# Causal attention: the row-maximum pass and the causal masks issued as four 128x32 column tiles, narrow diagonal blocks merged into one bank

## The reference: what is computed

```python
q, k, v = heads(x @ wq), heads(x @ wk), heads(x @ wv)   # 16 heads of 8 features
scores = einsum('bhqd,bhkd->bhqk', q, k)
scores = where(causal, scores, -inf)
attn = softmax(scores / sqrt(8), axis=-1)
ctx = einsum('bhqk,bhkd->bhqd', attn, v)
```

## Time and profile before

| | |
|---|---|
| time, median of 3 runs | 1314.45 us (1314.13 to 1315.17) |
| time of the profiled execution | 1314.37 us |
| its span in the profile | 1312.6 us |
| TensorE busy | 1186.3 us (90%), 8293 matmul records |
| TensorE weight loads | 461.7 us (35%) |
| VectorE busy | 1033.5 us (79%) |
| ScalarE busy | 668.8 us (51%) |
| GpSimd busy | 65.3 us (5%) |

### The profile page before, as it was taken

How to read it: one execution, slowest core, us unless ns; L and a number is a source line. 1 busy time by engine, 2 the same in 40 slices (tenths; PEclk the granted TensorE clock), 3 DMA queues, 4 the chain that set the end, 5 groups by cost and what they waited for, 6 DMA issues and landing times.

```text
span 1312.6 us, 21461 instructions
## 1 busy us (share of the span) xinstructions
PE 1186.3 (90%) x8293; PEld 461.7 (35%) x8293; DVE 1033.5 (79%) x2503; ACT 668.8 (51%) x861; POOL 65.3 (5%) x62
## 2 busy tenths in 40 slices
PE   1899968999999999999699979599999999999997
PEld 1455533222222222333355547232222222222336
DVE  8976487899999897875547566789999999877664
ACT  1322114555677667766332224145556667777663
POOL 5111010000000000000101000100000000000000
PEclk9999988999999999999799979799999999999999
DMA  4100141000000000000000000420000000000001
GB/s 147 33 1 1 48 121 57 1 2 1 2 1 1 2 1 1 1 1 2 1 0 1 1 0 25 146 57 1 1 2 1 1 1 1 1 1 2 1 2 33
DMA packets 23506, 23.26 MB, mean 18 GB/s; under 512 B 3134, under 2 KB 21220, under 8 KB 23404
## 3 DMA queue, kind: packets, MB, share of 16 engines
q1 hardware_dynamic: 22252, 18.73, 4.9%
q0 software_dynamic: 1152, 3.15, 0.9%
HBM read 13.20 MB, written 8.39 MB: 16 GB/s over the span
## 4 chain that ended last, share of the span: by engine, by line
PE 69%; DVE 25%; issue 2%; ACT 2%; DMA 1%; SPq 0%; DVEq 0%; ACTq 0%
PE psum L1182 19%; PE psum L1202 17%; DVE part_max L1317 14%; PE psum L442 9%; PE psum L1162 8%; PE psum L1169 4%; PE psum L466 2%; PE psum L898 2%; PE psum L1205 2%; PE psum L913 1%; DVE xn L167 1%; DVE norm_v L150 1%; PE psum L427 1%; DVE parts L838 1%; PE psum L1225 1%
## 5 line engine op out<-in xcount | busy, mean ns | idle before, releaser
L1317 DVE TENSOR_REDUCE part_max<-psum 128x1 f32<-128x512 f32 (+3 forms) x1280 | 703.5, 604 | 118.2 <-PE psum L1205 59.4
L1279 ACT ACTIVATE hidden<-psum 128x1024 f32<-128x1024 f32 (+3 forms) x640 | 542.4, 895 | 311.1 <-PE psum L1169 166.1
L1202 PE MATMUL psum<-k_slots,q_slots 128*128 128x512 f16 (+3 forms) x1280 | 396.8, 359 | 43.5 <-DVE part_max L1317 24.4
L1182 PE MATMUL psum<-hidden,v_aug 128*9 128x512 f32 (+3 forms) x2560 | 296.1, 535 | 0.0
L1202 PEld LDWEIGHTS psum<-k_slots,q_slots 128*128 128x128 f16 x1280 | 111.5, 97 | 402.0 <-DVE part_max L1317 320.0
L442 PE MATMUL psum<-parts,w_parts 128*128 128x512 f16 x768 | 177.6, 382 | 1.9 <-DVE parts L838 1.9
L1162 PE MATMUL psum<-q_slots,k_slots 32*128 32x512 f16 (+3 forms) x1280 | 163.9, 355 | 7.2 <-ACT hidden L1279 4.6
L1205 PE MATMUL psum<-ident_bf,later_keys 128*128 128x128 bf16 x512 | 111.0, 227 | 0.0
L442 PEld LDWEIGHTS psum<-parts,w_parts 128*128 128x128 f16 x768 | 73.2, 99 | 80.9 <-issue 3.0
L586 ACT CAST parts<-psum 128x512 f16<-128x512 f32 x64 | 37.2, 588 | 106.7 <-PE psum L427 106.7
L1162 PEld LDWEIGHTS psum<-q_slots,k_slots 32*128 32x128 f16 x1280 | 46.3, 91 | 109.4 <-issue 52.1
(11 more groups left out here) (168 smaller groups left out, 735.7 us busy)
## 6 DMA issues: line engine op xcount, KB each, us to landing
q_slots<-q_rows SPq DMA_DIRECT2D x8, 512.0 KB, 3.8
k_slots<-k_rows POOLq DMA_DIRECT2D x24, 128.0 KB, 4.1
q_rows<-parts SPq DMA_DIRECT2D x18, 128.0 KB, 2.7
k_rows<-parts SPq DMA_DIRECT2D x18, 128.0 KB, 2.4
q_slots<-in_L_ffn_W_dram SPq DMA_DIRECT2D x2, 1024.0 KB, 6.6
k_slots<-k_rows SPq DMA_DIRECT2D x8, 128.0 KB, 4.0
q_slots<-nm_parts SPq DMA_DIRECT2D x64, 4.0 KB
out_dram<-x_res SPq DMA_DIRECT2D x4, 256.0 KB, 2.3
```

Source lines behind the costliest of these rows:

```text
L1182: last = pe.matmul(psum[VW * h:VW * h + DH + 1, O_BANK, off:CH], v_aug[:, j, G * g + h, :], probs[:, (2 * n + h // 2) % NP, h % 2, off:CH] ...
L1202: last = pe.matmul(psum[:, bank, 0:w], q_slots[:, g, qb * P:(qb + 1) * P], k_slots[:, G * g + h, kc * CH:kc * CH + w], start=True, stop=kc ...
L1279: act.activation(probs[:, tile % NP, :, off:CH], psum[:, bank:bank + 2, off:CH], ACT.Exp, scale=scale).then_inc(exp_done, 1)
L1317: dve.tensor_reduce(dst, psum[:, bank, 0:w], axis=AX.X, op=ALU.max).then_inc(ring_read, 1)
```

## The change

1. `ring_item`: each maximum matmul, stationary 128x128, becomes four matmuls with stationary operands of 128x32 (32 queries each), moving the same keys, with their outputs on the four partition quarters of the bank. The mask matmul of a diagonal unit becomes four 128x32 ones likewise.
2. A diagonal unit of block 0 (128 wide) now holds 4 heads in one bank, one of block 1 (256 wide) 2 heads: 11 units per step on the diagonal in place of 16, 560 in a layer in place of 640. VectorE reduces such a bank with one instruction of 4 or 2 outputs, and one group of mask matmuls serves all heads of the bank.
3. The masks of the score tiles (`mask_tile`) are four 128x32 matmuls for each head, and are issued after both score tiles of the quad.
4. The ring items of a turn are cut in halves before and after `values`, no longer at three quarters.
5. `UNIT_FIXED, QUAD_FIXED` go from 64, 64 to 100, 500, and a unit's columns now count its mask: the number of units beside each quad shifts.

```diff
-        UNIT_FIXED, QUAD_FIXED = 64, 64
+        UNIT_FIXED, QUAD_FIXED = 100, 500
...
+                    heads = CH // unit_width(step, i, kc)
+                    units += [(step, i, kc, h, heads) for h in range(0, G, heads)]
...
+            return heads * (unit_width(step, i, kc) + (P if kc == step[1] else 0))
...
                                          start=True, stop=q not in diagonal)
-                    if q in diagonal:
-
-                        for par in range(2):
-                            last = pe.matmul(psum[:, S_BANKS + 2 * (tile % 2) + par, off:off + P],
-                                             ident_bf[:, :], later_keys[:, :], start=False, stop=True)
+                    if q not in diagonal:
+                        last.then_inc(scores_done, 1)
+
+                def mask_tile(q, pr):
+
+                    off = first_query(q)
+                    tile = 2 * quad_no[q] + pr
+                    for par in range(2):
+                        for m in range(COLS):
+                            last = pe.matmul(psum[rows32(m), S_BANKS + 2 * (tile % 2) + par, off:off + P],
+                                             ident_bf[:, rows32(m)], later_keys[:, :], start=False, stop=True)
                     last.then_inc(scores_done, 1)
...
-                        last = pe.matmul(psum[:, bank, 0:w], q_slots[:, g, qb * P:(qb + 1) * P],
-                                         k_slots[:, G * g + h, kc * CH:kc * CH + w], start=True, stop=kc < c)
+                        for a in range(heads):
+                            for m in range(COLS):
+                                last = pe.matmul(psum[rows32(m), bank, a * w:(a + 1) * w],
+                                                 q_slots[:, g, qb * P + m * SLOT:qb * P + (m + 1) * SLOT],
+                                                 k_slots[:, G * g + h0 + a, kc * CH:kc * CH + w],
+                                                 start=(a == 0), stop=(kc < c))
                         if kc == c:
-                            last = pe.matmul(psum[:, bank, i * P:w], later_keys[:, :], ident_bf[:, :],
-                                             start=False, stop=True)
+                            for m in range(COLS):
+                                last = pe.matmul(diagonal_part(psum[rows32(m), bank, 0:heads * w], heads),
+                                                 later_keys[:, rows32(m)], repeated(ident_bf, heads),
+                                                 start=False, stop=True)
...
-                    cuts = [0, 0, len(items) // 2 + len(items) // 4, len(items)]
+                    half = (len(items) + 1) // 2
                     if q:
                         score_tile(q, 0)
-                    for item in items[cuts[0]:cuts[1]]:
-                        ring_item(item)
-                    if q:
                         score_tile(q, 1)
-                    for item in items[cuts[1]:cuts[2]]:
+                    if q in diagonal:
+                        mask_tile(q, 0)
+                        mask_tile(q, 1)
+                    for item in items[:half]:
                         ring_item(item)
                     if previous:
                         values(previous)
-                    for item in items[cuts[2]:cuts[3]]:
+                    for item in items[half:]:
                         ring_item(item)
...
-                            dst = part_max[:, step_no[s] % 2, h, i, kc:kc + 1]
-                            w = CH if kc < s[1] else (i + 1) * P
-                            dve.tensor_reduce(dst, psum[:, bank, 0:w], axis=AX.X, op=ALU.max).then_inc(ring_read, 1)
+                            w = unit_width(s, i, kc)
+                            dve.tensor_reduce(part_max[:, step_no[s] % 2, h0:h0 + heads, i, kc],
+                                              psum[:, bank, 0:heads * w].rearrange("p (a k) -> p a k", a=heads),
+                                              axis=AX.X, op=ALU.max).then_inc(ring_read, 1)
```

More of the change, by code:

```diff
@@ L36 @@
 SLOT = 32
+COLS = P // SLOT
 MAX_ROW = TERMS * DH
@@ L1009, in macaron_layers, with unit_width @@
         SLACK = 3
-        UNIT_FIXED, QUAD_FIXED = 64, 64
+        UNIT_FIXED, QUAD_FIXED = 100, 500
         def quads_of(step):
             return [(step, j) for j in range(BPC * (step[1] + 1))]
+        def unit_width(step, i, kc):
+            return CH if kc < step[1] else (i + 1) * P
         def max_units_of(step):
-            return [(step, i, kc, h) for i in range(BPC) for kc in range(step[1] + 1) for h in range(G)]
+            units = []
+            for i in range(BPC):
+                for kc in range(step[1] + 1):
+                    heads = CH // unit_width(step, i, kc)
+                    units += [(step, i, kc, h, heads) for h in range(0, G, heads)]
+            return units
         def columns_of_quad(q):
@@ L1023, in columns_of_unit @@
         def columns_of_unit(u):
-            (_, c), i, kc, _ = u
-            return CH if kc < c else (i + 1) * P
+            step, i, kc, _, heads = u
+            return heads * (unit_width(step, i, kc) + (P if kc == step[1] else 0))
         def units_beside_quads():
@@ L1146, in attention_layer, with rows32, diagonal_part, repeated @@
                          for s in STEPS}
+            def rows32(m):
+                return slice(SLOT * m, SLOT * (m + 1))
+            def diagonal_part(rows, heads):
+                return rows.rearrange("p (a k) -> p a k", a=heads)[:, :, -P:]
+            def repeated(mask, heads):
+                return mask[:, :].rearrange("p (a k) -> p a k", a=1).broadcast_to([P, heads, P])
             @blk.tensor
@@ L1194, in ring_item @@
                     if kind == "scores":
-                        (g, c), i, kc, h = what
-                        if (g, i, kc, h) == (0, 0, 0, 0):
+                        (g, c), i, kc, h0, heads = what
+                        if (g, i, kc, h0) == (0, 0, 0, 0):
                             pe.wait_ge(q_landed[c], 16 if c else 16 * (G + 1))
@@ L1313, in _ @@
                         if kind == "scores":
-                            s, i, kc, h = what
-                            dst = part_max[:, step_no[s] % 2, h, i, kc:kc + 1]
-                            w = CH if kc < s[1] else (i + 1) * P
-                            dve.tensor_reduce(dst, psum[:, bank, 0:w], axis=AX.X, op=ALU.max).then_inc(ring_read, 1)
+                            s, i, kc, h0, heads = what
+                            w = unit_width(s, i, kc)
+                            dve.tensor_reduce(part_max[:, step_no[s] % 2, h0:h0 + heads, i, kc],
+                                              psum[:, bank, 0:heads * w].rearrange("p (a k) -> p a k", a=heads),
+                                              axis=AX.X, op=ALU.max).then_inc(ring_read, 1)
                         elif kind == "turned":
```

2 lines of the change are left out of this document (1 added, 1 removed).

## The result

The changed kernel takes 1227.73 us (median of 4 runs, 1224.66 to 1232.76) against 1314.29 us (4 runs, 1309.46 to 1315.17) for the kernel before. The ratio is 0.9352, 95% interval 0.931 to 0.9394: 6.5% less, some 85 us. Two further sets of runs of the same kernel gave ratios of 0.9333 and 0.9312.

What follows compares the result with a forecast made beforehand. The prediction took TensorE to set the pace, VectorE close behind in the first half. Relief kept, 26 us a layer less 1 for chunk 0, twice, gave 50 us off 1314: 1264 us, range 1244 to 1294.

Steps and rivals of the forecast that it cites:

- The price of a change of shape: TensorE: every change of matmul tile shape costs about 0.105 us; 763 changes a layer before, 355 after.
- A group of four tiles: Maximum and mask matmuls on TensorE: four 32-column f16 tiles of 512 columns run side by side in 0.22 us.
- Both slower rivals: TensorE: f16 strips no faster than f32, 1482 us, chance 0.07; matmul pairs can't be supplied, some 1450 us, chance 0.03.
- that of the narrow groups: Rival: 128-column groups held by four weight loads, or VectorE taking more; about 1285 us, 1279 to 1305, chance 0.16.
- The 5 ns a group on top: TensorE surcharge for each group of four column tiles, from weight-load starts 4 ns apart; 5.4 us a layer.
- ScalarE's idle time ahead of a diagonal quad: Wait before a diagonal quad's first exponential: about 0.65 us in the last steps, 1.15 us before the change.
- the sum: Six stages of a layer: net TensorE relief, cut where VectorE is nearly full, keeps 26 us, less 1 for chunk 0.
- Merging: Narrow diagonal units sharing a bank: fewer VectorE reductions save 0.4 us a step, or 6 us a layer.
- TensorE sets the pace: Attention stages before the change: TensorE's records cover 93 to 99% in the first three, with VectorE close behind.
- 0.3 us on some six turns and 1 us on two steps: ScalarE cost of later diagonal masks: some six 512- and 384-column turns from step (3,2) on, and chunk 0's two steps.
- moved units: New pace numbers shift units between turns: VectorE's work in six stages goes by +1.2, -2.2, -1.1, +1.4, -2.5, -2.5 us.
- all of TensorE's relief is kept: Rival: no relief is lost to VectorE, 35.6 us a layer; 1243 us, 1235 to 1250, chance 0.10.

## Why the prediction was wrong

What held, by its own steps:
- The price of a change of shape (0.105 us) and their count. The six stages lost 681 minus 316 changes, 38.3 us; the forecast had 37.9.
- A group of four tiles at 0.22 us; pairs supplied well below 60 ns. Both slower rivals and that of the narrow groups are out. The 5 ns a group on top have no place: no run shows them.
- ScalarE's idle time ahead of a diagonal quad, 0.61 us for 0.65. The stage of steps (2,2) and (3,2) lasts 54.5 us for "near 54".

What failed is the step of **the sum**: "In the first three the relief is about the room, and two engines that are both nearly full lose some time to each other; I keep 1.5 (its VectorE work grows), 4.5 and 7." The three stages gave 5.0, 8.9 and 11.6 us, the last three 3.3, 4.9 and 5.1 where I kept 2.7, 5.5 and 4.8. In all 38.8 for 26.

The loss that it names is real. Tiles alone lose 10 of 28 us, all parts but merging lose 8 of 38; the forecast lost 9.6 of 35.6. What was mis-sized is what stands against it. Merging was priced as 6 us of VectorE's work in a stage where TensorE was thought to set the pace, and the halved cut, item 4 of the change, not at all. They take 10 and 6 us of waiting from the six stages of the kernel before (table), 41 us of the whole between them, because TensorE already waited there: 31 us by the second count, 28 of them for a bank of the ring. The prediction's reading "TensorE sets the pace", which left that wait at nothing, is the root of it. In the changed kernel the two effects cancel: waiting is 35.5 us for 36.1, and the whole 38.3 us of the shape is kept. That they cancel so closely is chance, and the waiting is not the same one: less for VectorE, more for ScalarE. Of the latter the prediction had 0.3 us on some six turns and 1 us on two steps; ahead of scores there are 7 us more a layer, so this term was too small, against the direction of the miss. The account of the 36 us between 1264 and 1228: 25 in the six stages of the two layers (12.9 and 12.3; of the first, 10.2 in waiting, 5.4 for the surcharge that did not exist, and 2.7 the other way in moved units and the count), 8 in steps (0,0) and (1,0), for which I had nothing (29.5 to 24.4 us in the first layer, 27.4 to 24.4 in the second), and 2 elsewhere. In these two steps many units meet few quads; the sum put nothing on their relief and 1 us a layer against it for chunk 0, since it was made for the six stages. Some 2 of the 8 us go with the clock: the clock granted to TensorE was 0.88 in this stretch of the first layer of the kernel before (202.9 to 232.4), and 1.00 in its second layer, which took 27.4 us, and in both layers of the changed kernel. From 207.7 to 214.6 us it was at the lower of its two levels, 1.2 of 2.4 GHz, after 4.7 us in which TensorE was busy for 3.4. That the change keeps it from falling there is not shown.

The rival nearest to it, "all of TensorE's relief is kept", names what became of the relief, but with 1243 us (1235 to 1250) it missed as well, and for the same reason: it, too, ended at the forecast's 35.6 us a layer.

Shown by runs: tiles, merging and cut each save time by themselves, 42, 25 and 16 us, and the masks' place as the last part 12 to 17. They sum to 95 to 100, where the kernel with exactly these four saves 93; with intervals of 2 to 5 us on each, and one part taken last and not alone, so close a sum is in part luck. Shown too: waiting for VectorE was in the kernel before. Argued only: that fuller banks work by carrying VectorE through the values; a ring of four banks would test it, and was not run; the kernel uses banks 0 to 3 for scores, 4 for the values and 5 to 7 for the ring. Open: which turns make the halved cut pay, and why the old pace numbers are 4.5 us better.

## What to carry to other kernels

A covered timeline is no proof that an engine sets the pace: subtract from a stage its columns and its counted fixed costs, start to start, and what is left is waiting, even at 99% by records. Then ask of each wait which matmul stands behind it: here it told VectorE's share from ScalarE's. Where two engines hand banks to each other in a short ring, price what each bank holds and where the long foreign piece of work stands between them; here that was worth as much as the relief of the busier engine. And give a column-tiled neighbour its own shape, since it is the change that costs: one shape left over in between (64 for 32) gave all of it back.

## What was not expected of the hardware

- A change between tile shapes costs 96 to 115 ns at the median of nearly every pair seen: 32x128, 128x128, 128x64 and 128x32, in both directions. A matmul of the same shape follows 3 ns after the columns of the one before where it follows at once (0.216 us at 512 columns, 0.109 at 256, 0.055 at 128); many of the maxima follow 13 ns after (0.226 us), before and after the change.
- Four heads of a score tile run side by side, and two alone take as long as four: two of 512 columns need 0.320 us to their mask, four 0.32 to the next shape. A mask between them costs the room of two heads besides the change of shape.
- Four column tiles of one group run at the full pace down to 128 columns (55 ns a group of four pairs, 14 ns a pair in a burst). The Trainium skill ("TensorE: Matmul & The Clock Gate", Part 3) gives three such tiles 2.38 times the pace of one after another; here four f16 tiles of 512 columns take together 0.216 us, no more than one 128x128 matmul of as many columns does. The pace of one column tile alone was not run.
- VectorE takes 686 ns for a reduction of 512 columns to four maxima and 681 for one to a single maximum; the number of outputs costs nothing, as these forms of the changed kernel show (busy us, mean ns | idle before):

```profile
L1349 DVE TENSOR_REDUCE part_max<-psum 128x1 f32<-128x512 f32 x896 | 555.7, 681 | 29.3 <-PE psum L1231 13.4 <-PE psum L1237 11.4
...
L1349 DVE TENSOR_REDUCE part_max<-psum 128x2 f32<-128x512 f32 x64 | 42.6, 685 | 6.7 <-PE psum L1237 6.0
...
L1349 DVE TENSOR_REDUCE part_max<-psum 128x4 f32<-128x512 f32 x32 | 21.9, 686 | 10.1 <-PE psum L1237 9.9
```
